# A GRU kernel's spline tail: slices written instead of added, and the spline moved into the recurrence's block

## The chip, the cores and the metric

The kernel runs on one core of one Trainium2 chip. The metric is the device time of one execution in microseconds (us); lower is better. The engines are TensorE (PE), VectorE (DVE), ScalarE (ACT), GpSimd (POOL) and SyncE (SP); SP and POOL issue nearly all transfers here.

## The reference

`x` has 4 batches, 1024 positions and 1024 features. A GRU with 1024 states runs over the positions, starting from `cond_2048`:

```python
gi = x @ W_ih + b_ih;  gh = h @ W_hh + b_hh
r = sigmoid(i_r + h_r);  z = sigmoid(i_z + h_z);  n = tanh(i_n + r * h_n)
h = (1 - z) * n + z * h            # hs[t] = h
```

Its states `hs` go through a routed spline layer. Each token is normalised (`xf = layernorm(hs) * gamma + beta`); the signs of `xf` choose one of 64 experts (best of 8 clusters, then best of 8 experts in it). Expert `k` owns the 16 features `16k` to `16k + 15`. `lo` and `hi` are the least and the greatest value of that slice over all tokens that chose the expert:

```python
u = clip((x_slice - lo) / (hi - lo + 1e-8), 0, 1 - 1e-6)
g = int(u * 16)                                    # cell of the 16-cell grid
delta = (base[k, j, g] + slope[k, j, g] * (u * 16 - g)) * output_scale[k]
out = x + hs;  out[token, 16k : 16k + 16] += delta
```

## The kernel before

The 1024 positions are cut into 16 chunks that run side by side (each warmed up over the 44 positions before it), so a step of the recurrence works on 16 x 4 = 64 columns in two sets (`s` = 0, 1) of 32. A `tile` is two steps of all columns: 128 tokens; there are `TILES` = 32 of them. Phases, in order of time:

- `input_product`: `x @ W_ih` into a scratch in HBM, and preparations.
- `recurrence`, one block of engine programs: warm-up steps, then `one_pass` over the 32 tiles. Tiles up to 21 run in `FULL` mode (three products with split weights), tiles 22 to 31 in `DIFFS` mode (one product, with stored sums of the warm-up added). Around the steps of tile `i` each engine does the routing work of the tiles before: ScalarE sums and squares (`act_sum`, `act_squares`, L734 to L740), GpSimd makes `rstd` and `shift` (`pool_scale`, L1109 to L1113), ScalarE normalises (L744), VectorE applies gamma and beta (`dve_signed`, L903 and L905), ScalarE takes signs (L749), VectorE finds the expert (`dve_route`, L920 to L932), TensorE turns the one-hot row (`pe_turn`, L636), ScalarE keeps it as `hits_t` (L753). GpSimd's `pool_keep` makes the row index and gathers the token's own slice of `hs` (L1134, 128 rows of 64 bytes), `pool_pick` copies it to `picks` (L1141), and `pool_add` adds the whole tile of `hs` to `y` by an accumulating transfer (L1120), after SP has copied `x` there (L1248, `begin_y`).
- `dve_ends` (L959 to L978) turns the picks into `records` (the slices of `xf`) and folds their ends into `ends`, in three batches of tiles and four parts each. The last batch is done after the last tile.
- `passes` (L563 to L573) wraps `one_pass`: after the first pass every engine loads `flag` (L566), and jumps over up to 16 further passes when it is 0, as it is here. Behind the jump the block ends, with a drain and a barrier (L573).
- `spline`, a second block: TensorE turns `ends` (L1414), VectorE reduces them to the experts' `lo` and `hi` and splits them into exact parts (L1452 to L1455, with `split_exactly`, L410 to L414). TensorE brings, through the one-hot rows, per-token values (`per_token`, L1430) and the curves of the token's expert (`curves(g)`, L1423; nine groups of 4 or 3 tiles; seven banks, in two halves: `curves(g)` waits until group `g - 2` is used). VectorE finds the cells (`cells(n)`, for tiles 0 to 3, 4 to 17 and 18 to 31) and, for each group, chooses among the 16 cells by halving (`choose(g)`, L1494) and makes `delta` (L1497 to L1500). GpSimd adds `delta` to `y`:

```python
            for g, (a, b) in enumerate(GROUPS):
                pool.wait_ge(delta_ready, g + 1)
                for i in range(a, b):
                    pool.indirect_dma_start(out=y_slices[:], out_offset=bass.IndirectOffsetOnAxis(ap=row_i[:, i:i + 1], axis=0),
                                            in_=delta[:, i], in_offset=None, compute_op=ALU.add).then_inc(added, 16)
            pool.wait_ge(added, 16 * TILES)
```

Each engine runs its own program in order; semaphores (`wait_ge`, `then_inc`) are the only order between engines. `curve_used` is sent by `value` (L1498), before the last multiplication.

Of the kernel before, what the change touches and what calls it, by code (L numbers as in the profile page):

```python
# [4 lines left out]
F32 = mybir.dt.float32  # L5
# [8 lines left out]
P = 128  # L14
# [7 lines left out]
SETS = 2  # L22
# [394 lines left out]
def recurrence(nc, ctx, t, h0, gi_dram, sums_dram, states_dram, hs_dram, x_rows, y_rows, tables, late_w):  # L417
# [3 lines left out]

    def pb(name, shape, dt=F32):
        return ctx.enter_context(nc.psum_tensor(name, shape, dt))
# [27 lines left out]
    pick_now = out_room[:, at + 7 * NT + 2 * ENDS_MOST:at + 7 * NT + 2 * ENDS_MOST + SLICE]  # L451
    affine_left = xhat[0:NT, D // 2:D // 2 + 4 * SLICE].rearrange("t (a f) -> t a f", a=2)
# [16 lines left out]
    n_act = sb("n_act", [P, SETS, QF])  # L469
    z_old = sb("z_old", [P, SETS, QF])  # L470
    new_n = n_sum
# [32 lines left out]
    affine_banks = affine[:].rearrange("p i f -> p (i f)")  # L504
    late_acc = [hit_bank[:], misc_bank[:], affine_banks[:, 0:512], affine_banks[:, 512:1024]]
# [67 lines left out]
    with nc.Block() as block:  # L573
# [75 lines left out]
        def _(pe):  # L649
# [45 lines left out]
            passes(pe, one_pass)  # L695

        def act_step(act, it, u, s, turns, mode=FULL, after_gates=None, after_tanh=None):
            n = steps_to(it, u)
            if mode == DIFFS:
                act.wait_ge(rz_done[s], n)  # L700
                nc.scalar.activation(rz[:, s], rz_bank[s][:], ACT.Sigmoid, scale=UNSCALE).then_inc(rz_ready[s], 1)
# [131 lines left out]
        def dve_step(dve, it, u, s, seeds, mode=FULL, after_sums=None, after_old=None):  # L833
# [7 lines left out]
            else:  # L841
                dve.wait_ge(rz_done[s], n)
                dve.wait_ge(gi_loaded[s][u], it * 64 + 64)
                nc.vector.scalar_tensor_tensor(out=sums[:, s, 0:RZ], in0=rz_bank[s][:], scalar=UNSCALE, in1=gi[:, s, u, 0:RZ],  # L844
# [136 lines left out]
        def _(dve):  # L981
# [50 lines left out]
            def one_pass(p, first):  # L1032
# [71 lines left out]
            passes(dve, one_pass)  # L1104

# [17 lines left out]
        def pool_keep(pool, T, tile):  # L1123
# [10 lines left out]
            pool.indirect_dma_start(out=pick_now[:], out_offset=None,  # L1134
                                    in_=hs_dram.rearrange("i q p (k j) -> (i q p k) j", j=SLICE),
                                    in_offset=bass.IndirectOffsetOnAxis(ap=row_now[:, 0:1], axis=0)).then_inc(picked, 16)

        def pool_pick(pool, T, tile):
            pool.wait_ge(picked, T * 16)
            pool.sem_inc(wait_carrier, 1)  # L1140
            nc.gpsimd.tensor_copy(t["picks"][:, one(tile)].rearrange("p o j -> p (o j)"), pick_now[:]).then_inc(pick_kept, 1)  # L1141

        @block.gpsimd
        def _(pool):
# [22 lines left out]
            def one_pass(p, first):  # L1167
# [190 lines left out]
def spline(nc, ctx, t, y_slices):  # L1358

    def sb(name, shape, dt=F32):  # L1360
        return ctx.enter_context(nc.sbuf_tensor(name, shape, dt))
# [25 lines left out]
    delta = sb("delta", [P, TILES, SLICE])  # L1387
# [7 lines left out]
    tok_bank = ctx.enter_context(nc.psum_tensor("tok_bank", [P, 512], F32))  # L1395
    turn_bank = tok_bank[0:NT, 4 * TILES:4 * TILES + 2 * P]
    curve_bank = ctx.enter_context(nc.psum_tensor("curve_bank", [P, 7, 512], F32))
# [3 lines left out]
    math_step, delta_ready, added = (sem(n) for n in ("math_step", "delta_ready", "added"))  # L1401
# [7 lines left out]
    with nc.Block() as block:  # L1409

        @block.tensor
        def _(pe):
# [215 lines left out]
```

## Time and profile before

| | us |
|---|---|
| median of 3 runs (2497.98 to 2498.7) | 2498.41 |
| the profiled execution | 2499.93 |
| its span, first to last instruction | 2498.1 |
| TensorE busy in the span | 2350.0 |
| VectorE busy | 1300.9 |
| ScalarE busy | 660.3 |
| GpSimd busy | 191.2 |

Busy times are of the profiled execution alone. They are averages over stages with different limits, so stretches have to be read one by one. The mean granted clock of TensorE is 0.966 of full speed.

### The profile page before, as it was taken

To read this page: it belongs to the slowest core of one execution; us is meant where nothing else is said; L and a number is where in the kernel's file an instruction comes from. 1 tells how busy PE (TensorE), PEld (TensorE's weight loads), DVE (VectorE), ACT (ScalarE), POOL (GpSimd) and SP (SyncE) were. 2 spreads that over 40 slices of the span, in tenths; PEclk is the share of its full clock that TensorE was granted. 3 is DMA by queue.
4 is the path that set the end of the run, shared out by engine and by line. 5 is a ranking of instruction groups with operands and counts; after the bars stand their busy time and mean duration, and the time that the engine had idled before them with its cause. 6 is when DMAs were issued, how large, how long until landed. Compare 5 with 4: busy or idle time off the path is not lost. (4 is left out here: it accounts for less than half of the span.)

```text
span 2498.1 us, 83612 instructions
## 1 busy us (share of the span) xinstructions
PE 2350.0 (94%) x35300; PEld 1285.8 (51%) x35300; DVE 1300.9 (52%) x2682; ACT 660.3 (26%) x1333; POOL 191.2 (8%) x376
## 2 busy tenths in 40 slices
PE   7999999999999989999999999999999999977734
PEld 3444444444444445455666666666666666544411
DVE  4322121212123357776666655666666666888865
ACT  3200000000001123333333323333333333355510
POOL 0000000000000000000000000111111111122217
PEclk9999999999999999999999999999999999999955
DMA  7693131313133445453444444444444444477712
GB/s 237 208 325 127 51 127 51 127 51 126 51 144 110 155 145 156 137 152 120 139 134 134 134 130 111 116 116 116 117 118 118 117 117 118 128 231 230 219 43 4
DMA packets 179895, 330.35 MB, mean 132 GB/s; under 512 B 27856, under 2 KB 89728, under 8 KB 178752
## 3 DMA queue, kind: packets, MB, share of 16 engines
q1 hardware_dynamic: 145360, 267.53, 34.0%
q10 hardware_dynamic: 24192, 44.05, 4.7%
q0 software_dynamic: 10240, 17.31, 4.7%
q8 instruction: 76, 1.25, 0.2%
q14 instruction: 27, 0.22, 0.0%
HBM read 222.13 MB, written 156.77 MB: 152 GB/s over the span
## 5 line engine op out<-in xcount | busy, mean ns | idle before, releaser
L580 PE MATMUL rz_bank<-w_hi,hi 128*32 128x512 f16 x6912 | 429.9, 392 | 49.4 <-DVE hi L879 37.0
L312 DVE SCALAR_TENSOR_TENSOR out_stage<-acc,bias_row 128x512 f32<-128x512 f32 x168 | 116.0, 690 | 624.4 <-PE acc L370 624.4
L368 PE MATMUL acc<-w_hi,x_even 128*128 128x512 f16 x768 | 291.8, 380 | 13.4 <-DVE x_even L304 11.3
L580 PEld LDWEIGHTS rz_bank<-w_hi,hi 128*32 128x32 f16 x6912 | 178.6, 99 | 234.4 <-DVE hi L879 45.3
L369 PE MATMUL acc<-w_hi,x_even 128*128 128x512 f16 x768 | 291.8, 380 | 0.0
L370 PE MATMUL acc<-w_lo,x_even 128*128 128x512 f16 x768 | 291.7, 380 | 0.0
L705 ACT ACTIVATE rz<-sums 128x512 f32<-128x512 f32 x176 | 110.9, 630 | 535.2 <-DVE sums L844 534.9
L844 DVE SCALAR_TENSOR_TENSOR sums<-rz_bank,stage 128x512 f32<-128x512 f32 x176 | 121.3, 689 | 239.3 <-PE rz_bank L580 239.2
L580 PE MATMUL rz_bank<-w_lo,hi 128*32 128x512 f16 x4096 | 243.2, 379 | 0.0
L580 PE MATMUL rz_bank<-w_hi,lo 128*32 128x512 f16 x4096 | 243.2, 379 | 0.0
L580 PE MATMUL n_bank<-w_hi,hi 128*32 128x256 f16 x6912 | 227.9, 274 | 0.0
L368 PE MATMUL acc<-w_hi,x_keep 128*128 128x512 f16 x576 | 218.3, 379 | 1.9 <-issue 1.9
L370 PE MATMUL acc<-w_lo,x_keep 128*128 128x512 f16 x576 | 218.3, 379 | 0.0
L369 PE MATMUL acc<-w_hi,x_keep 128*128 128x512 f16 x576 | 218.3, 379 | 0.0
L580 PEld LDWEIGHTS n_bank<-w_hi,hi 128*32 128x32 f16 x6912 | 186.2, 98 | 53.6 <-issue 5.3
L580 PEld LDWEIGHTS rz_bank<-w_lo,hi 128*32 128x32 f16 x4096 | 109.6, 97 | 84.2
L580 PEld LDWEIGHTS rz_bank<-w_hi,lo 128*32 128x32 f16 x4096 | 109.6, 97 | 84.1
L710 ACT ACTIVATE n_act<-n_sum 128x256 f32<-128x256 f32 x216 | 90.2, 417 | 178.7 <-DVE n_sum L857 178.7
L580 PE MATMUL n_bank<-w_lo,hi 128*32 128x256 f16 x4096 | 134.0, 273 | 0.0
L580 PE MATMUL n_bank<-w_hi,lo 128*32 128x256 f16 x4096 | 134.0, 273 | 0.0
L368 PEld LDWEIGHTS acc<-w_hi,x_even 128*128 128x128 f16 x768 | 75.3, 98 | 104.8 <-issue 12.1
L580 PEld LDWEIGHTS n_bank<-w_lo,hi 128*32 128x32 f16 x4096 | 109.6, 97 | 29.5
(191 smaller groups left out, 2661.6 us busy)
## 6 DMA issues: line engine op xcount, KB each, us to landing
stage<-gi_scratch SPq DMA_DIRECT2D x704, 96.0 KB
gi_scratch<-out_stage ACTq DMA_DIRECT2D x168, 256.0 KB, 2.0
stage<-sums_scratch SPq DMA_DIRECT2D x40, 512.0 KB
stage<-in_xT SPq DMA_DIRECT2D x32, 512.0 KB, 6.3
y<-in_x_rows SPq DMA_DIRECT2D x32, 512.0 KB, 4.4
hs_scratch<-h SPq DMA_DIRECT2D x128, 128.0 KB
x_keep<-hs_scratch SPq DMA_DIRECT2D x32, 512.0 KB, 3.9
y<-hs_scratch POOLq DMA_DIRECT2D x32, 512.0 KB, 7.7
```

The lines of the kernel that those rows point to most:

```text
L312: nc.vector.scalar_tensor_tensor(out=out_stage[:, tb], in0=acc[e % BANKS][:], scalar=UNSCALE, in1=bias_row[:].rearrange("p q f -> p (q f)" ...
L368: nc.tensor.matmul(acc[e % BANKS][:], hi, wh, start=k == 0, stop=False)
L369: nc.tensor.matmul(acc[e % BANKS][:], lo, wh, start=False, stop=False)
L370: last = nc.tensor.matmul(acc[e % BANKS][:], hi, wl, start=False, stop=k == KB - 1)
L580: last = nc.tensor.matmul(bank[q * COLS:(q + 1) * COLS, 0:b - a], state[:, s, j], w[:, j, q * QW + a:q * QW + b], start=first and j == 0, ...
L705: nc.scalar.activation(rz[:, s], sums[:, s, 0:RZ], ACT.Sigmoid).then_inc(rz_ready[s], 1)
L710: nc.scalar.activation(n_act[:, s], n_sum[:, s], ACT.Tanh).then_inc(n_ready[s], 1)
L844: nc.vector.scalar_tensor_tensor(out=sums[:, s, 0:RZ], in0=rz_bank[s][:], scalar=UNSCALE, in1=gi[:, s, u, 0:RZ], op0=ALU.mult, op1=ALU.add ...
```

## The change

The spline no longer has a block of its own: `spline` returns three functions, `pe_spline`, `dve_spline` and `pool_spline`, and each engine's program in the recurrence's block calls its own behind `passes`. Its tiles lie in `w_lo`, its PSUM banks are the recurrence's. A new semaphore `ends_ready` stands between VectorE's last ends and TensorE's transposes; `curves(0)` now precedes that wait. The scatter writes the slice and no longer accumulates; what it has to hold, `x + hs + delta`, VectorE makes with one more addition per group from `base`. `base` is gathered in the main pass: `pool_keep` issues a second gather, of `x`, and `pool_pick` adds the two. GpSimd waits for the last add to `y` before it leaves the pass. In the last tile's work the order changes: GpSimd keeps tile 30 and scales before it adds to `y`, and VectorE does `dve_ends(p, 1, 1)` before `dve_signed`.

```diff
 def recurrence(...):
+    x_now = out_room[:, at + 8 * NT:at + 8 * NT + SLICE]
+    base = t["base"]
...
-    rz_bank = [pb(f"rz_bank{s}", [P, 512]) for s in range(SETS)]
-    n_bank = [pb(f"n_bank{s}", [P, 512]) for s in range(SETS)]
-    hit_bank = pb("hit_bank", [P, 512])
-    misc_bank = pb("misc_bank", [P, 512])
-    affine = pb("affine", [P, TILES, 2 * SLICE])
+    banks = t["banks"]
+    rz_bank = [banks[:, s] for s in range(SETS)]
+    n_bank = [banks[:, SETS + s] for s in range(SETS)]
+    hit_bank, misc_bank = banks[:, 4], banks[:, 5]
+    affine = banks[:, 6:8].rearrange("p b f -> p (b f)").rearrange("p (i f) -> p i f", f=2 * SLICE)
...
             passes(pe, one_pass)
+            pe_spline(pe)
...
+                dve_ends(dve, p, 1, 1)
                 dve_signed(dve, T)
-                dve_ends(dve, p, 1, 1)
                 dve_route(dve, T)
...
             passes(dve, one_pass)
+            dve_spline(dve)
...
         def pool_keep(pool, T, tile):
...
-            pool.indirect_dma_start(out=pick_now[:], out_offset=None,
-                                    in_=hs_dram.rearrange("i q p (k j) -> (i q p k) j", j=SLICE),
-                                    in_offset=bass.IndirectOffsetOnAxis(ap=row_now[:, 0:1], axis=0)).then_inc(picked, 16)
+            for now, rows in ((pick_now, hs_dram), (x_now, x_rows)):
+                pool.indirect_dma_start(out=now[:], out_offset=None,
+                                        in_=rows.rearrange("i q p (k j) -> (i q p k) j", j=SLICE),
+                                        in_offset=bass.IndirectOffsetOnAxis(ap=row_now[:, 0:1], axis=0)).then_inc(picked, 16)
...
         def pool_pick(pool, T, tile):
-            pool.wait_ge(picked, T * 16)
+            pool.wait_ge(picked, T * 32)
             pool.sem_inc(wait_carrier, 1)
+            nc.gpsimd.tensor_tensor(base[:, one(tile)].rearrange("p o j -> p (o j)"), x_now[:], pick_now[:], ALU.add)
...
-                with pool.Fori(2, TILES + 1) as i:
+                with pool.Fori(2, TILES) as i:
                     tile(i, True)
+                T = p * TILES + TILES
+                pool_keep(pool, T - 1, TILES - 2)
+                pool_scale(pool, T, TILES - 1)
+                pool_add(pool, T, TILES - 1)
+                pool_pick(pool, T - 1, TILES - 2)
                 pool_keep(pool, p * TILES + TILES, TILES - 1)
                 pool_pick(pool, p * TILES + TILES, TILES - 1)
+                pool.wait_ge(y_added, p * (TILES * 16) + TILES * 16)
+                pool.sem_inc(wait_carrier, 1)
 
             passes(pool, one_pass)
+            pool_spline(pool)
...
 def spline(nc, ctx, t, y_slices):
 
+    room = t["w_lo"][:].rearrange("p k n -> p (k n)")
...
-    delta = sb("delta", [P, TILES, SLICE])
+    delta = rise
...
-            for e in range(2):
-                ins = nc.tensor.transpose(turn_bank[:, e * P:(e + 1) * P], t["ends"][:, e], t["ident"][:])
-            ins.then_inc(ends_turned, 1)
...
+    def pe_spline(pe):
...
+        curves(0)
+        pe.wait_ge(ends_ready, 1)
+        for e in range(2):
+            ins = nc.tensor.transpose(turn_bank[:, e * P:(e + 1) * P], t["ends"][:, e], t["ident"][:])
+        ins.then_inc(ends_turned, 1)
+        pe.wait_ge(rows_split, 1)
+        per_token(*CELLS[0])
...
+    def dve_spline(dve):
...
+        dve.sem_inc(ends_ready, 1)
+        dve.wait_ge(ends_turned, 1)
...
-                nc.vector.tensor_tensor(delta[:, s], value[:, s], wide(per_tok[:, s, 0]), ALU.mult).then_inc(delta_ready, 1)
+            step(nc.vector.tensor_tensor(delta[:, s], value[:, s], wide(per_tok[:, s, 0]), ALU.mult))
+            nc.vector.tensor_tensor(delta[:, s], t["base"][:, s], delta[:, s], ALU.add).then_inc(delta_ready, 1)
...
-                                            in_=delta[:, i], in_offset=None, compute_op=ALU.add).then_inc(added, 16)
+                                        in_=delta[:, i], in_offset=None).then_inc(added, 16)
...
 def program(...):
+        t["base"] = ctx.enter_context(nc.sbuf_tensor("base", [P, TILES, SLICE], F32))
+        t["banks"] = ctx.enter_context(nc.psum_tensor("banks", [P, BANKS, 512], F32))
...
-        t["records"] = ctx.enter_context(nc.sbuf_tensor("records", [P, TILES, SLICE], F32))
+
+        t["records"] = t["picks"]
...
-                       y, tables, late_w)
-        with ExitStack() as phase:
-            spline(nc, phase, t, y.rearrange("i q p (k j) -> (i q p k) j", j=SLICE))
+                       y, tables, late_w, *spline(nc, phase, t, y.rearrange("i q p (k j) -> (i q p k) j", j=SLICE)))
```

## Rows read from the trace of the kernel before

**Rows 1.** Windows: stretch, length, then busy us (count) per engine, clock, DMA share.
```profile
1520.00:2180.00 660.00, 658.09 (x16058) 429.31 (x16046) 446.91 (x970) 244.14 (x504) 81.03 (x204) 1.00 0.45 118
2180.00:2384.00 204.00, 153.15 (x2626) 79.10 (x2626) 170.25 (x417) 113.13 (x278) 45.92 (x100) 0.90 0.76 220
2433.00:2475.00 42.00, 32.24 (x75) 10.30 (x73) 33.98 (x91) 0.00 (x0) 34.37 (x22) 0.50 0.22 5
```

**Rows 2.** The chain that ended last: start us, us, engine, what, line.
```profile
2419.55 0.60 PE tok_bank L1414 x2
...
2441.75 1.54 POOL y L1513
...
2492.02 1.55 POOL y L1513
```

**Rows 3.** Timeline of the spline: start us, us, engine, line, what, idle before.
```profile
2432.69 0.22 DVE L1500 TENSOR_TENSOR delta<-value,per_tok 128x64 f32<-128x64 f32 x1
...
2441.29 18.10 PE L1423 MATMUL curve_bank<-curve_parts,late_ring 64*128 64x512 bf16 x42 [3.28 <-DVE value L1498]
...
2471.18 2.75 DVE L1494 COPY_PREDICATED curve_bank<-in_upper,curve_bank 128x1024 f32<-128x1024 int32 x4 [2.14 <-PE curve_bank L1423]
...
2474.49 0.22 DVE L1500 TENSOR_TENSOR delta<-value,per_tok 128x64 f32<-128x64 f32 x1
```

**Rows 4.** Groups of GpSimd's indirect transfers, and their medians of us to landing.
```profile
L1513 POOL DMA_INDIRECT y<-delta,row_i x32 | 49.9, 1559 | 33.9 <-DVE delta L1500 24.7 <-issue 9.1
...
L1134 POOL DMA_INDIRECT late_out<-hs_scratch,row_now x30 | 33.5, 1117 | 19.2 <-issue 19.2
...
late_out<-hs_scratch,row_now POOLq DMA_INDIRECT x32, 2.5
y<-delta,row_i POOLq DMA_INDIRECT x32, 3.0
```

**Rows 5.** Timeline: the last row part, and the first per-token products.
```profile
2421.60 0.16 DVE L414 CAST row_parts<-row_left 64x4 bf16<-64x4 f32 x1
...
2425.18 0.50 PE L1430 MATMUL tok_bank<-row_parts,late_ring 64*128 64x4 bf16 x12
```

**Rows 6.** Queue instructions by line: duration ns, then first and last start us.
```profile
L566 PEldq COMPARE_BRANCH  x1: 3640/3640/3640, 2406.2 to 2406.2; - x1
...
L566 DVEq COMPARE_BRANCH  x1: 56/56/56, 2415.6 to 2415.6; - x1
...
L573 DVEq DRAIN  x1: 76/76/76, 2419.2 to 2419.2; - x1
```

**Rows 7.** Timeline behind the last tile's steps.
```profile
2393.28 0.15 DVE L1095 CAST flag<-misc_bank 1x1 int32<-1x1 f32 x1 [0.68 <-PE misc_bank L690]
...
2395.16 0.19 POOL L1113 TENSOR_TENSOR shift<-neg_mean,rstd 128x1 f32 x1 [0.16 <-POOL rstd L1111]
...
2396.66 1.23 DVE L903 TENSOR_TENSOR x_keep<-x_keep,gamma_s 128x1024 f32<-128x1024 f32 x1 [3.23 <-ACT x_keep L744]
...
2401.63 1.22 DVE L920 TENSOR_REDUCE late_out<-bias_row 128x64 f32<-128x1024 bf16 x1
...
2409.62 0.19 POOL L1141 COPY picks<-late_out 128x16 f32<-128x16 f32 x1 [2.69 <-DMA late_out<-hs_scratch,row_now]
...
2413.96 0.22 DVE L978 TENSOR_TENSOR ends<-late_out,ends 128x64 f32<-128x64 f32 x1
```

**Rows 8.** Timeline: two rows of a `FULL` tile, then three of a `DIFFS` tile.
```profile
1913.44 0.19 POOL L1113 TENSOR_TENSOR shift<-neg_mean,rstd 128x1 f32 x1 [0.17 <-POOL rstd L1111]
...
1918.47 1.23 ACT L744 ACTIVATE x_keep<-x_keep,shift,rstd 128x1024 f32<-128x1024 f32 x1
...
2293.72 1.16 POOL L1134 DMA_INDIRECT late_out<-hs_scratch,row_now  x1 [0.46 <-issue]
...
2296.30 0.19 POOL L1113 TENSOR_TENSOR shift<-neg_mean,rstd 128x1 f32 x1 [0.16 <-POOL rstd L1111]
...
2299.48 1.22 DVE L903 TENSOR_TENSOR x_keep<-x_keep,gamma_s 128x1024 f32<-128x1024 f32 x1
```

More of the change, by code:

```diff
@@ L1 @@
+import math
 import concourse.bass as bass
@@ L1358, in spline @@
 def spline(nc, ctx, t, y_slices):
+    room = t["w_lo"][:].rearrange("p k n -> p (k n)")
+    taken = [0]
     def sb(name, shape, dt=F32):
-        return ctx.enter_context(nc.sbuf_tensor(name, shape, dt))
+        halves = math.prod(shape[1:]) * (1 if dt == BF16 else 2)
+        flat = room[0:shape[0], taken[0]:taken[0] + halves].bitcast(dt)
+        taken[0] += (halves + 15) // 16 * 16
+        dims = "abc"[:len(shape) - 1]
+        return flat.rearrange(f"p ({' '.join(dims)}) -> p {' '.join(dims)}", **dict(zip(dims, shape[1:])))
     def sem(name):
@@ L1394, in spline @@
     CELLS = ((0, 4), (4, 18), (18, TILES))
-    tok_bank = ctx.enter_context(nc.psum_tensor("tok_bank", [P, 512], F32))
+    tok_bank = t["banks"][:, 7]
     turn_bank = tok_bank[0:NT, 4 * TILES:4 * TILES + 2 * P]
-    curve_bank = ctx.enter_context(nc.psum_tensor("curve_bank", [P, 7, 512], F32))
+    curve_bank = t["banks"][:, 0:7]
     ends_turned, row_step, rows_split, tok_ready, tok_known, curve_ready, curve_used = (
         sem(n) for n in ("ends_turned", "row_step", "rows_split2", "tok_ready", "tok_known", "curve_ready", "curve_used"))
-    math_step, delta_ready, added = (sem(n) for n in ("math_step", "delta_ready", "added"))
+    math_step, delta_ready, added, ends_ready = (sem(n) for n in ("math_step", "delta_ready", "added", "ends_ready"))
     def curves_of(g):
@@ new lines, in pe_spline, with curves, per_token @@
+    def pe_spline(pe):
+        def curves(g):
+            if g >= 2:
+                pe.wait_ge(curve_used, g - 1)
+            a, b = GROUPS[g]
+            for i in range(a, b):
+                for part in range(3):
+                    ins = nc.tensor.matmul(curve_bank[:, 4 * (g % 2) + i - a], hits_t[:, i], curve_parts[:, part],
+                                           start=part == 0, stop=part == 2)
+            ins.then_inc(curve_ready, 1)
+        def per_token(a, b):
+            for i in range(a, b):
+                for part in range(3):
+                    ins = nc.tensor.matmul(tok_bank[:, i * 4:(i + 1) * 4], hits_t[:, i], row_parts[:, part],
+                                           start=part == 0, stop=part == 2)
+            ins.then_inc(tok_ready, 1)
+        curves(0)
[5 more added lines that the diff above has]
+        per_token(*CELLS[0])
+        pe.wait_ge(tok_known, 1)
+        per_token(CELLS[0][1], TILES)
+        for g in range(1, len(GROUPS)):
+            curves(g)
@@ L1518, in constants, with pool_spline @@
+    def pool_spline(pool):
+        for g, (a, b) in enumerate(GROUPS):
+            pool.wait_ge(delta_ready, g + 1)
+            for i in range(a, b):
+                pool.indirect_dma_start(out=y_slices[:], out_offset=bass.IndirectOffsetOnAxis(ap=row_i[:, i:i + 1], axis=0),
+                                        in_=delta[:, i], in_offset=None).then_inc(added, 16)
+        pool.wait_ge(added, 16 * TILES)
+    return pe_spline, dve_spline, pool_spline
 def constants(nc, t):
```

152 lines of the change are left out of this document (57 added, 95 removed).

## The prediction

> **What bounds the kernel now.** I read the windows view first, to cut the run into stages [rows 1]. From 1520 to 2180 us TensorE is busy 658 of 660 us at full clock: the main pass over tiles 1 to 21 (the `FULL` mode) is TensorE's. From 2180 to 2384 (the `DIFFS` tiles 22 to 31) TensorE is busy 153 of 204 and VectorE 170. From 2433 on TensorE's granted clock is 0.50, its 1.2 GHz level; behind the last tile, from about 2384, lies a tail of 114 us. The first two stages can only lose by this change unless a wait in them goes; the gain has to come from the tail.
>
> In the tail I read the chain that ended last [rows 2]. It starts at the spline's first transposes at 2419.55, goes through one group of curve products, VectorE's `cells(0)`, `choose(0)`, `cells(1)`, `choose(1)`, and from 2441.75 it is GpSimd alone: 28 issues of the accumulating scatter of L1513. The reader is to see the cadence: 1.55 us of issue and 0.30 us between, 1.86 us each. VectorE made its last `delta` at 2474.71 [rows 3], 17.3 us before the last scatter began, so VectorE and TensorE are not the bound there.
>
> The spans: the profiled execution took 2499.93 us for a span of 2498.1, so 1.8 us lie outside; the median of the runs is 2498.41, 1.5 below the profiled one. I sum differences on the profiled one and take them from the median. A difference of 0.2% is 5.0 us, about what a measurement of this kernel tells from none.
>
> **1. The scatter's price.** `compute_op=ALU.add` goes; 32 scatters of 128 rows of 64 bytes stay. The trace has no plain scatter. Its nearest rows are the accumulating scatter, 1559 ns mean, and the plain gather of the same 128 x 64 bytes on the same engine, 1117 ns mean [rows 4]. The landing is 3.0 us after the issue's start for the one and 2.5 for the other. So an issue costs between 1.10 and 1.55 us. I take 1.10: the gather differs in the side that has the index, the scatter in a second read of the destination for the sum, and the latter is what the change takes away. The 0.30 us between issues stays. Cadence: 1.40 (or 1.86 at the other end). A page of the Trainium skill speaks for less: "DMA: Bandwidth & Descriptors" (its table at the top) says that a transfer under 512 bytes is read-modify-write anyway. No row tells whether that hits a plain 64-byte write; by it the landing would stay 3.0 instead of 2.5 and the end come 0.5 us later.
>
> **2. What the scatters then wait for.** From the first `delta` (2432.91, end) to the last (2474.71) VectorE takes 41.8 us [rows 3]. The change puts one addition (`base` to `delta`, 128x64) in each of nine groups: 0.22 + 0.03 us by L1500's row [rows 3]. Replayed against TensorE: `curve_used` is sent before the multiplication by the scale, so TensorE is not delayed; the groups whose curves VectorE waits for anyway (4, and 8 with 2.14 us of waiting [rows 3]) absorb it. What is left at the last group is 0.26 us that the extra addition of group 4 puts on `cells(2)` and what follows, and its own 0.26: 42.3 us from first to last `delta`. GpSimd has 24 scatters to issue from group 1's arrival (its first began at 2441.75 [rows 2], 8.8 us behind group 0's `delta`) to group 8's: 24 x 1.40 = 33.6 us against 42.3 - 8.8 = 33.5. So at 1.40 GpSimd just keeps up, and the last scatter starts at 0.3 (hop) + 42.3 + 3 x 1.40 = 46.8 us after the first `delta`; before it was 2492.02 - 2432.91 = 59.1. That is **-12.3**. A cheaper scatter than 1.40 would bring only its last three. At 1.86 nothing is gained here (+0.3, the extra addition in group 1).
>
> **3. Behind the last scatter.** Before, 6.1 us from its start to the end. With the landing at 2.5 instead of 3.0: **-0.5**. The drain and what else lies behind stay.
>
> **4. Curves early.** `curves(0)` (12 products, 5.2 us at the 0.43 us of 42 in 18.10 [rows 3]) stood between the transposes and the per-token products, which began at 2425.18 though VectorE had `row_parts` at 2421.76 [rows 5]. Now it runs while VectorE still makes the ends: TensorE's conditional jump begins at 2406.2 and takes 3.64 us [rows 6], then 5.2 us: done by 2415. The per-token products follow `row_parts` at once (a hop of 0.06): 3.42 - 0.07 = **-3.35**. The extra addition in `choose(0)` gives back **+0.26**.
>
> **5. The block's boundary.** VectorE's last step ends at 2414.18 [rows 7] and the transposes start at 2419.52. One would book these 5.3 us as the barrier of the block. The queue rows tell otherwise [rows 6]: VectorE loads the flag and compares it until 2415.65, and its next instruction, the drain, is at 2419.2: 3.55 us behind the taken branch. TensorE's branch shows the same as its own length, 3.64 us. The branch over the conditional passes is still there and is as far, so 5.0 of the 5.3 stay; the drain and the semaphores go: **-0.2** (0.1 is the new `ends_ready` hop). The Trainium skill says this of a taken branch ("Runtime: NRT & Kernel Launch", Instruction fetch mechanics): a target outside the fetched window has to be fetched by DMA first. By it and by the row the boundary gives 0.2; by the barrier alone it would give 5.2.
>
> **6. The recurrence's end, reordered** [rows 7]. VectorE idled 3.23 us from the flag (2393.43) until `xhat` came. `dve_ends(1, 1)` filled the 2.5 us from the end of `dve_signed` (2396.66 and two operations of 1.23) to the routing at 2401.63; now it fills that idle time, to about 2396.0. GpSimd now keeps tile 30 before it adds to `y`, so `shift` has neither that issue nor a wait for its input before it: it came at 2395.35 and is wanted, for `dve_signed` at 2396.0, by 2394.7. I take it that it gets there. Then `dve_signed` ends at 2398.5, ScalarE's signs take at most the 1.23 us of its pass over the same shape (L744, [rows 8]), and the routing starts at 2399.7 instead of 2401.63: 1.9 us sooner. But GpSimd now gathers twice for the last tile too: from the routing's start to the kept picks (2409.81) it took 8.2 us, now 8.2 + 1.40 (second issue) + 0.25 (the addition, by the copy's 0.19 and a pause) = 9.85 from 2399.7, so 2409.55. The last ends wait for the picks. Of 1.9 us **-0.25** stays.
>
> **7. The second gather in the main pass.** It stands in `pool_keep`, before `pool_scale` on GpSimd's queue; behind `pool_scale` waits ScalarE's normalisation (L744), and in ScalarE's queue the next gate behind that. In `FULL` tiles `shift` is there 4.8 us before its use [rows 8], 1.4 is hidden. In `DIFFS` tiles GpSimd goes from the gather straight to `var_eps`, so the gather is already what `shift` waits for, and 1.17 + 0.30 = 1.47 us more comes through. `shift` ends at 2296.49; normalisation (1.23) must end before VectorE reads at 2299.48: slack 1.68 [rows 8]. 1.47 fits, with 0.2 left; with the 0.46 us pause that the first gather has before it, it would just fit. If the second issue cost what the accumulating scatter does, 1.86, 0.18 us would come through in each of ten tiles: +2. I take 0 and keep +2. The additions of `base` lie in GpSimd's idle time (46 of 204 us busy [rows 1]). The wait for `y_added` on GpSimd ends long before the first `delta`.
>
> `delta = rise`, `records = picks`, the tiles in `w_lo` and the renamed banks cost nothing: same shapes, same engines.
>
> **Sum.** -12.3 - 0.5 - 3.35 + 0.26 - 0.2 - 0.25 = -16.3: 2498.41 - 16.3 = **2482.1 us**.
>
> **Rivals.**
> A. *The plain scatter costs what the accumulating one did.* For: it is the side with the index that may set the price, and no row has that alone. Then steps 2 and 3 give +0.3 and 0: -3.2, 2495.2 us. A price between (issues of 1.25 to 1.45 us) makes GpSimd the bound from group 1 on, with 27 cadences: 2.7 us for each 0.1, so 2486 to 2492.
> B. *The boundary goes*: the code behind the branch is fetched already when VectorE gets there, against the 3.55 and 3.64 us of [rows 6]. For: part of these could be the next block's code, which now is laid elsewhere. Then 3.5 us more: 2478.6.
> C. *Slower: the second gather in the `DIFFS` tiles.* It comes a few us behind the 512 KB add to `y`, on the same queue. If GpSimd had to wait for room there, `shift` would be late, and VectorE with it: per tile (cost - 1.68), ten times. To eat 16.3 + 5.0 us it would need to cost 3.8 us, to only come out slower 3.3 us. Against: the first gather, at the same place, costs 1.16 there [rows 8] and 1.12 in the mean [rows 4].
> D. *TensorE gets its full clock back in the tail*, because `curves(0)` now fills an idle stretch. Then groups 4 and 8 need not wait; group 8's 2.14 us is the most that it gives. Against: 42 products in 18.1 us did not raise it from 0.50 [rows 3].
>
> **Chances.** The forecast with its small unknowns (D and up to +2 of step 7 among them) 0.65; A in full 0.12; A in part 0.13; B 0.07; C 0.03. The likeliest case's own range is 2479.5 to 2485. For the whole, from B's 2477.5 up to 2490.5, which leaves out A in full, a little of A in part, and C. Faster by over 0.2% (below 2493.4): 0.65 + 0.13 + 0.07 = 0.85; within 0.2%: A in full, less a little, 0.11; slower 0.04.
>
> **What would show it.** Step 1: L1513's row, mean about 1.1 us and landings of 2.5; near 1.55 is A. Step 2: the last scatters wait for VectorE's last addition, not for "issue"; last scatter about 46.5 us behind the first. Step 4: the per-token products begin within 0.2 us of the last `row_parts`. Step 5: from the last end to the transposes 5.1 us; under 3 is B. Step 6: the routing's start 1.9 us sooner, the last ends only 0.25. Step 7: the `DIFFS` tiles take 204 us as before, and L903 with no idle time before it; if it waits for L744, the slack was used up. What makes me wrong most easily is the price of a plain scatter, the one number no row has.

## The result and the profile after

The changed kernel takes **2480.85 us** (median of 6 runs, 2479.73 to 2484.99) beside 2498.55 (6 runs, 2497.57 to 2498.82) for the kernel before: ratio 0.9933, 95% interval 0.9923 to 0.9943, so 17.7 us less. The forecast was 2482.1. The profiled execution took 2479.73 us for a span of 2478.2.

Four numbers cut a profile: the start of GpSimd's first add to `y` (the main pass is then at its first tile), the start of the first scatter, the start of the last, and the span.

| | first `y` add | first scatter | last scatter | span |
|---|---|---|---|---|
| before | 1519.63 | 2433.21 | 2492.02 | 2498.08 |
| after | 1516.46 | 2426.42 | 2472.47 | 2478.16 |

The scatters' stretch went from 58.81 to 46.05 us (-12.8), what lies behind it from 6.06 to 5.69 (-0.4), and the stretch from the first add to `y` to the first scatter from 913.6 to 910.0 (-3.6). The other 3.2 us lie in the setup, which the change does not touch; three other profiles of the changed kernel have 1518.5, 1518.2 and 1517.6 there, so most of that part is chance.

The windows view of after, with the columns of [rows 1]:
```profile
1520.00:2180.00 660.00, 655.94 (x15990) 425.33 (x15982) 448.48 (x974) 246.29 (x508) 103.78 (x243) 1.00 0.45 118
2180.00:2384.00 204.00, 138.72 (x2610) 75.43 (x2602) 169.80 (x414) 113.07 (x274) 57.52 (x120) 0.97 0.76 219
2427.00:2469.00 42.00, 31.20 (x73) 9.92 (x71) 34.72 (x96) 0.00 (x0) 27.20 (x29) 0.50 0.03 6
```
Of the work, only GpSimd's changes in the first two stretches (81 to 104 us, 46 to 58: the second gather and `base`). TensorE's 139 us instead of 153 in the second stretch go with its granted clock, 0.97 in this execution and 0.90 in the one of before. That did not make the `DIFFS` tiles shorter: 20.6 us in both. In the tail the clock stays at 0.50.

The scatters in the grouped view, with the columns of [rows 4]:
```profile
L1530 POOL DMA_INDIRECT y<-w_lo,row_i x32 | 31.3, 978 | 35.7 <-DVE w_lo L1518 27.2 <-issue 8.5
```
The view of one line has its instructions' duration in ns (least, median, most), their first and last start and the time to landing. Of the scatter's line and of the gathers':
```profile
L1530 POOL DMA_INDIRECT y<-w_lo,row_i x32: 955/962/1173, 2426.4 to 2472.5; - x32
...
DMA to landing us min/median/max: 2.1/2.1/2.7
...
L1138 POOL DMA_INDIRECT late_out<-hs_scratch,row_now x32: 1067/1115/1204, 1560.6 to 2401.5; - x32
L1138 POOL DMA_INDIRECT late_out<-in_x_rows,row_now x32: 953/958/1525, 1562.1 to 2402.9; - x32
```
Against [rows 4] a scatter costs 978 instead of 1559 ns, and lands 2.1 instead of 3.0 us after its issue starts. With the 0.30 us between issues, the cadence (from one issue's start to the next's) is 1.27.

The timeline of the spline after, to be laid beside [rows 2] and [rows 3]:
```profile
2425.91 0.23 DVE L1518 TENSOR_TENSOR w_lo<-base,w_lo 128x64 f32<-128x64 f32 x1
...
2435.15 0.96 POOL L1530 DMA_INDIRECT y<-w_lo,row_i  x1 [3.90 <-DVE w_lo L1518]
...
2455.55 0.21 DVE L1518 TENSOR_TENSOR w_lo<-base,w_lo 128x48 f32<-128x48 f32 x1
...
2456.03 0.96 POOL L1530 DMA_INDIRECT y<-w_lo,row_i  x1 [2.99 <-DVE w_lo L1518]
...
2468.06 0.22 DVE L1518 TENSOR_TENSOR w_lo<-base,w_lo 128x64 f32<-128x64 f32 x1
...
2472.47 0.96 POOL L1530 DMA_INDIRECT y<-w_lo,row_i  x1 [0.30 <-issue]
```
L1518 is now the last operation of each group. GpSimd waits for it twice, at group 1 (3.90 us) and at group 5 (2.99); from 2456.03 on it issues the last 14 scatters without a wait. The last `delta` ends at 2468.28, and three cadences behind it and a hop of 0.3 (from VectorE's end to GpSimd's start) give 2472.4, which is where the last scatter is anyway. So both engines set the end: VectorE up to group 5, and from there either.

The timeline ahead of the spline, TensorE and one row of VectorE, to be laid beside [rows 5] and [rows 7]:
```profile
2405.31 5.30 PE L1436 MATMUL banks<-curve_parts,late_ring 64*128 64x512 bf16 x12 [4.29 <-issue]
...
2410.56 0.22 DVE L980 TENSOR_TENSOR ends<-late_out,ends 128x64 f32<-128x64 f32 x1
...
2415.86 0.63 PE L1450 MATMUL banks<-ident,ends 128*64 128x128 f32 x2 [5.25 <-DVEq L1467]
...
2418.15 0.48 PE L1443 MATMUL banks<-w_lo,late_ring 64*128 64x4 bf16 x12 [1.66 <-DVE w_lo L416]
```
`curves(0)` is done at 2410.6, before the last end is. The per-token products follow the last row part (started at 2417.93) at 2418.15. From the last end to the transposes there are 5.08 us, 5.34 before.

### The profile page after: what moved, and what is told of

Its sections match the earlier page's. It is cut to its first block and busy times, and to the rows that moved or that the text cites. A ratio compares the mean times of both kernels' runs of the same rounds, so it can differ in the third digit from the quotient of the medians.

```text
span 2478.2 us, 83692 instructions
## 1 busy us (share of the span) xinstructions
PE 2335.3 (94%) x35300; PEld 1277.8 (52%) x35300; DVE 1303.3 (53%) x2691; ACT 661.4 (27%) x1333; POOL 210.6 (8%) x440
## 5 line engine op out<-in xcount | busy, mean ns | idle before, releaser
L581 PE MATMUL banks<-w_hi,hi 128*32 128x512 f16 (+1 forms) x13824 | 605.0, 328 | 55.7 <-DVE hi L881 43.0
L581 PEld LDWEIGHTS banks<-w_hi,hi 128*32 128x32 f16 x13824 | 359.8, 97 | 284.8 <-DVE hi L881 53.7
L581 PE MATMUL banks<-w_hi,lo 128*32 128x512 f16 (+1 forms) x8192 | 354.9, 326 | 0.0
L581 PE MATMUL banks<-w_lo,hi 128*32 128x512 f16 (+1 forms) x8192 | 354.9, 326 | 0.0
L370 PE MATMUL acc<-w_hi,x_even 128*128 128x512 f16 x768 | 291.7, 380 | 13.5 <-DVE x_even L306 11.1
L581 PEld LDWEIGHTS banks<-w_lo,hi 128*32 128x32 f16 x8192 | 217.8, 97 | 115.0
L581 PEld LDWEIGHTS banks<-w_hi,lo 128*32 128x32 f16 x8192 | 217.8, 97 | 115.0
L846 DVE SCALAR_TENSOR_TENSOR sums<-banks,stage 128x512 f32<-128x512 f32 x176 | 121.5, 690 | 238.3 <-PE banks L581 238.2
L370 PEld LDWEIGHTS acc<-w_hi,x_even 128*128 128x128 f16 x768 | 75.3, 98 | 104.7 <-issue 11.7
L371 PEld LDWEIGHTS acc<-w_hi,x_even 128*128 128x128 f16 x768 | 75.3, 98 | 90.6 <-issue 0.6
L871 DVE TENSOR_TENSOR n_sum<-not_z,n_act 128x256 f32<-128x256 f32 x216 | 92.6, 429 | 36.8 <-ACT n_act L712 36.8
L886 DVE TENSOR_TENSOR h<-n_sum,z_old 128x256 f32<-128x256 f32 x216 | 90.3, 418 | 20.4 <-DVE n_sum L871 7.4
```

What stands on the lines that cost most here:

```text
L370: nc.tensor.matmul(acc[e % BANKS][:], hi, wh, start=k == 0, stop=False)
L371: nc.tensor.matmul(acc[e % BANKS][:], lo, wh, start=False, stop=False)
L581: last = nc.tensor.matmul(bank[q * COLS:(q + 1) * COLS, 0:b - a], state[:, s, j], w[:, j, q * QW + a:q * QW + b], start=first and j == 0, ...
L871: nc.vector.tensor_tensor(new_n[:, s], not_z[:, s], n_act[:, s], ALU.mult).then_inc(new_n_ready[s], 1)
L886: nc.vector.tensor_tensor(h_new, new_n[:, s], z_old[:, s], ALU.add).then_inc(h_ready[s], 1)
```

## Experiments

The runs were made in three sets, each on a chip of its own (1st, 2nd, 3rd). On which chip the first measurement was made is not recorded. Ratios are against the kernel before on the same chip. A `FULL` tile's time is the mean from the add to `y` of tile 2 to that of tile 21, a `DIFFS` tile's from tile 22 to tile 30, counted from 0; the expectations below leave out the two longer tiles at the end of the `FULL` mode and have 31.5 and 32.5 for 31.75 and 32.73. "Behind it" is from the start of the last scatter to the end of the span.

| run | median us | ratio, 95% interval | us per `FULL` tile | first to last scatter | behind it |
|---|---|---|---|---|---|
| changed, 1st chip | 2500.47 | 1.0009 (1.0000 to 1.0018) | 32.73 | 46.20 | 5.69 |
| accumulating, one gather | 2495.16 | 0.9986 (0.9977 to 0.9996) | 31.76 | 58.82 | 8.80 |
| plain scatter in before | 2484.58 | 0.9942 (0.9927 to 0.9958) | 31.76 | 45.70 | 5.21 |
| curves late | 2503.49 | 1.0022 (1.0013 to 1.0031) | 32.73 | 46.04 | 5.69 |
| changed, 2nd chip | 2481.14 | 0.9929 (0.9914 to 0.9944) | 31.74 | 46.19 | 5.69 |
| one gather | 2484.11 | 0.9939 (0.9924 to 0.9954) | 31.75 | 46.15 | 7.86 |
| `hs` gathered twice | 2481.35 | 0.9930 (0.9915 to 0.9945) | 31.76 | 46.19 | 5.69 |
| `x` behind the scale | 2479.80 | 0.9924 (0.9910 to 0.9937) | 31.76 | 46.20 | 5.73 |
| changed, 3rd chip | 2480.28 | 0.9927 (0.9912 to 0.9942) | 31.75 | 46.19 | 5.69 |
| no branch | 2475.90 | 0.9909 (0.9894 to 0.9924) | 31.78 | 46.21 | 5.68 |
| three gathers | 2496.34 | 0.9992 (0.9982 to 1.0001) | 31.77 | 46.19 | 7.48 |
| ends sent early | 2479.39 | 0.9922 (0.9908 to 0.9935) | 31.76 | 46.20 | 5.73 |

### The scatter's form alone, both ways

In the kernel before, the scatter made plain (its slices then hold the spline's part alone, without `x + hs`):
```
-    in_=delta[:, i], in_offset=None, compute_op=ALU.add)
+    in_=delta[:, i], in_offset=None)
```


> The kernel before, with compute_op taken from its scatter and nothing else; its slices hold delta alone, without x and hs. Theory (price of accumulating): issues of 0.96 us and a landing of 2.1 us here too; the first scatter starts at the same place, VectorE's groups come when they came, so the last scatter is set by group 5 (its delta ended 29.3 us behind group 0's) plus 13 x 1.27 or by the last delta (41.8) plus 3 x 1.27: 46 us from first to last instead of 58.8, and 0.35 less behind it. 2498.5 - 12.8 - 0.35 = 2485.3. Rival (place): issues stay 1.55 and the time 2498.5.

Measured: 13.5 us less than before, first to last scatter 45.70. In the changed kernel, the accumulating scatter put back, with the second gather and `base` taken out, so that the sum is whole again:

> The changed kernel with the scatter accumulating again, and without the second gather, the addition that makes base and the nine additions of base; it computes the same output. Theory: what the change brought in the scatters was the price of accumulating, 0.59 us of each. Then issues are 1.55 us again, 1.86 from one to the next, the scatters are GpSimd's from group 1 on, 58.6 us from first to last, and 6.1 from the last to the end: 12.6 + 0.4 us slower than the changed kernel, less about 1.5 for the last tile's single gather and 0.7 for the main pass: 2480.85 + 10.8 = 2491.7. Rival: the scatters are cheaper because they stand in the recurrence's block or because their data and indices lie elsewhere; then they stay at 0.96 us and the time is 2479.

Measured: 2495.16, 2.9 us less than before; the scatters cost what they did before:
```profile
L1528 POOL DMA_INDIRECT y<-w_lo,row_i x32 | 49.9, 1560 | 30.3 <-DVE w_lo L1516 21.2 <-issue 9.1
```
So the price belongs to the form of the scatter (plain 0.98 us also in the old code, accumulating 1.56 also in the new). By itself the form is worth 13.5 us in the old code, beside the 17.7 of the whole change in the first measurement, whose profile has 13.1 for the scatters' stretch and what lies behind it. The miss of the second run is not in the scatters (58.82, as expected) but behind them: 8.80 us instead of 6.06. The queue rows name it. GpSimd's last drain, by itself, in that run, in the run with one gather, and in the changed kernel:
```profile
L574 POOLq DRAIN  x1: 5338/5338/5338, 2489.2 to 2489.2; - x1
```
```profile
L574 POOLq DRAIN  x1: 5338/5338/5338, 2478.6 to 2478.6; - x1
```
```profile
L574 POOLq DRAIN  x1: 3174/3174/3174, 2474.8 to 2474.8; - x1
```
It goes with the program: 5338 ns in both kernels with one gather in the block, 3174 in all with two gathers at L1138, 4971 with three, 3215 with the second gather placed elsewhere; before, 5297 at the end of the recurrence's block, with its one gather, and 2660 at the end of the spline's own. There the longer one cost nothing: it was over at 2416.0, ahead of VectorE's drain at 2419.2. In the changed kernel's single block GpSimd's drain is the last thing that runs. What in the program sets it was not tried.

### Curves late

```
     def pe_spline(pe):
-        curves(0)
         pe.wait_ge(ends_ready, 1)
```
with the call put back between the transposes and the per-token products.

> The changed kernel with curves(0) moved back between the transposes and the per-token products. Theory: the 5.3 us of 12 products come back into the chain from the transposes to the first scatter, of which 1.6 us lie beside VectorE's reductions and splits, less hops: 3.4 us slower, 13.9 from the transposes to the first scatter instead of 10.6; all behind it unchanged: 2484.3. Rival: the products may be slower or faster after the idle time that arises (TensorE's granted clock is 0.50 in both); then the 10.6 moves by another amount, or the scatters' stretch of 46.1 does.

Measured: 3.0 us more than the changed kernel on the same chip. From the transposes to the first scatter 13.94 us instead of 10.56, the 3.4 that step 4 says.

### The changed kernel on other chips

> The changed kernel once more, beside the kernel before on the same chip. In the first pair of profiles the main pass began 3.2 us sooner in the changed kernel (first add to y at 1516.5 against 1519.6), in a part that the change does not touch. Theory 1 (chance of one execution): it begins at about 1519.5 here, or anywhere between, and the tail's terms (last ends to transposes 5.1, transposes to first scatter 10.6, first to last scatter 46.1, then 5.7) are the same within 0.1 us. Theory 2 (the new layout of the tiles makes the setup faster): it begins at 1516.5 again.

Measured: nothing gained, 2500.47 us. The tail is as it was (46.20 and 5.69). The 20 us are in the main pass: the first add to `y` at 1518.5, the one of tile 21 at 2204.5 instead of 2182.6. The timeline of one `FULL` tile on this chip, GpSimd and TensorE:
```profile
1855.43 1.10 POOL L1138 DMA_INDIRECT late_out<-hs_scratch,row_now  x1 [0.69 <-issue]
...
1856.84 0.96 POOL L1138 DMA_INDIRECT late_out<-in_x_rows,row_now  x1 [0.30 <-issue]
...
1857.48 0.13 PEld L581 LDWEIGHTS banks<-w_lo,hi 128*32 128x32 f16 x6 [0.56 <-issue]
...
1858.23 0.80 PEld L581 LDWEIGHTS banks<-w_lo,hi 128*32 128x32 f16 x19 [0.62 <-issue]
```
The weight loads stop twice, next to the issue of the second gather, with no semaphore that the trace names ("issue"), at a granted clock of 1.00. Each `FULL` tile has these two stops, and is 0.98 us longer for them (32.73 against 31.75), 20 tiles. The two kernels with one gather on this chip have none; curves late, with two, has them. The same kernel on two more chips:

> The changed kernel, a third time. In its second run its FULL tiles took 32.5 us instead of 31.5, with two stops of 0.65 and 0.7 us in TensorE's weight loads in each tile, the first within 0.05 us of the second gather's issue; in its first run no such stop. Theory 1 (it goes with the chip or with where the data lie on it): here it is one of the two, 2481 or 2500, for all executions alike. Theory 2 (chance from execution to execution): single times on both sides.

> The changed kernel once more, beside the runs of this call, on whichever chip this is. Two profiles of it so far show FULL tiles of 31.5 us and a ratio of 0.993, one shows 32.5 us with two stops of TensorE's weight loads (0.65 and 0.70 us) in each and a ratio of 1.001. Theory 1 (the stops go with the chip): all profiles and times of this call show the one or the other. Theory 2 (they come and go by chance with each run): the runs of this kernel in this call are spread by over 10 us.

Measured: 2481.14 and 2480.28 us, no stops, 31.75 us a tile, as in the first measurement. The runs of each set agree (2480.32 to 2481.61, 2479.18 to 2481.11; on the chip with the stops 2499.14 to 2504.96), so the stops go with the set, that is with the chip or with something that stayed the same on it (where the data lie, say), and not with the single run. One chip of three had them, and it was met in one set only.

### What the second gather costs

One gather (the second left out, `base` made from `hs` alone, so `x` is missing in the slices), and `hs` gathered twice (the same, with both issues):
```
-            for now, rows in ((pick_now, hs_dram), (x_now, x_rows)):
+            for now, rows in ((pick_now, hs_dram), (x_now, hs_dram)):
```


> The changed kernel without the second gather (base becomes twice the slice of hs, so the written slices lack x); every other part stays. Theory A (the second gather makes TensorE's stops): no stop in any FULL tile wherever it runs, tiles of 31.5 us; the last tile's picks come 0.7 to 1.4 us sooner: 2479.5. Theory B (the stops come from the new layout of tiles and banks, or from the longer program, and only coincide with the gather): where the changed kernel has them beside it, this has them too.

> The changed kernel with the second gather reading hs again instead of x (the written slices lack x). Theory A1 (what stops TensorE is the second indirect issue itself, or two of them back to back): it goes as the changed kernel beside it, 2481 or 2500. Theory A2 (it is the source x, where it lies in memory): no stops here even where the changed kernel has them, 2481.

Measured: one gather 2484.11, 3.0 us slower than with two; `hs` twice 2481.35, the same as the changed kernel. The 3.0 do not come from the gather's own place. 2.2 us are the drain above (7.86 against 5.69). The first add to `y` is 3.6 us later in that profile, in the setup; but the profiled execution took 2485.78, and two of the four took 2482.6 and 2482.8, so how much of this is in the median is open. From the add of tile 30 to the first scatter, one gather is 1.5 us faster (56.36 against 57.87). The `DIFFS` tiles are 20.58 us with one gather and with two. On this chip the tensor gathered from makes no difference. There were no stops to remove here, and on the chip that has them neither kernel was tried. Nor does the tensor set an issue's price. Two issues of one tile, both from `hs`:
```profile
1751.64 1.10 POOL L1138 DMA_INDIRECT late_out<-hs_scratch,row_now  x1 [0.70 <-issue]
1753.05 0.95 POOL L1138 DMA_INDIRECT late_out<-hs_scratch,row_now  x1 [0.30 <-issue]
```
The one right behind another costs 0.95; with the gather of `x` moved away from that of `hs` (the run with `x` behind the scale) it costs 1.06 in such a tile.

Three gathers (a third, `x` again, into a buffer that nothing reads):
```
-            for now, rows in ((pick_now, hs_dram), (x_now, x_rows)):
+            for now, rows in ((pick_now, hs_dram), (x_now, x_rows), (x_more, x_rows)):
```


> The changed kernel with a third gather of each tile, x's slice once more, right behind the second, into a buffer that nothing reads; nothing else differs. Theory 1 (rival C's mechanism: GpSimd's gathers are what shift waits for in the DIFFS tiles, with a slack of 1.68 us of which the second gather used up 1.27): the third costs 1.27 again, 0.85 us of it comes through in each of ten DIFFS tiles, TensorE waits for the normalisation there, and the kernel takes 8 us more than the changed kernel of this call (plus up to 1.2 for the last tile's picks). FULL tiles stay at 31.5 (slack 4.8). Theory 2 (the normalisation is not on the path in the DIFFS tiles even then): within 1.5 us of the changed kernel. If this is a chip with the stops of TensorE: they come with every gather behind the first (three in each FULL tile, 33.0 us or more) or stay two (32.5).

Measured: 16.1 us more than the changed kernel, twice what was expected. A `DIFFS` tile takes 21.59 instead of 20.56 us. ScalarE's and VectorE's rows of the normalisation in the window 2180 to 2384 (busy us, mean ns, then idle us before them and for whom), first with two gathers (the first measurement), then with three:
```profile
L746 ACT ACTIVATE x_keep<-x_keep,shift,rstd 128x1024 f32<-128x1024 f32 x10 | 12.4, 1240 | 2.5 <-POOL shift L1116 1.4
...
L905 DVE TENSOR_TENSOR x_keep<-x_keep,gamma_s 128x1024 f32<-128x1024 f32 x10 | 12.2, 1215 | 0.7 <-ACT x_keep L746 0.7
```
```profile
L747 ACT ACTIVATE x_keep<-x_keep,shift,rstd 128x1024 f32<-128x1024 f32 x9 | 11.2, 1241 | 14.9 <-POOL shift L1117 14.9
...
L906 DVE TENSOR_TENSOR x_keep<-x_keep,gamma_s 128x1024 f32<-128x1024 f32 x9 | 11.0, 1225 | 8.4 <-ACT x_keep L747 8.4
```
The third gather costs 1.26 us (from one issue's start to the next's, 2299.66 to 2300.92 in the timeline), and 1.03 of it come through in each tile: the second had left 0.23 us of slack. With three gathers VectorE waits 0.93 us in each tile. With two it waits 0.7 us once in ten tiles in the first measurement, and not at all in the profiles of the 2nd and 3rd chip. The granted clock, 0.90 in this stretch with three gathers and 0.98 with two on this chip, is not the cause: it was 0.90 in the kernel before too, with tiles of 20.6 us. From the add of tile 21 to that of tile 30 the profile is 8.3 us longer than the changed kernel's; from there to the add of tile 31 another 4.3 (27.0 against 22.7), where `shift` is late again, to the first scatter 1.1, and the drain gives 1.8. Rival C's mechanism is real and was 0.2 us away.

### The branch

The conditional passes (the correction passes that put the running sums right) taken out:
```
         body(0, True)
-        eng.wait_ge(pass_judged, 1)
-        eng.sem_inc(wait_carrier, 1)
-        with eng.If(eng.value_load(flag[0:1, 0:1], min_val=0, max_val=P) > 0):
-            ...
```


> The changed kernel with the branch over the conditional passes taken out, and with it these passes, which set the running sums right where tiles are not in order; nothing else differs. The prediction's step 5 says that 5.0 us between VectorE's last end and the first transpose are VectorE's load of the flag, its comparison (1.5 us) and the 3.55 us behind the taken branch. Theory 1 (it is the branch and the fetch behind it): from the last end to the transposes 0.2 instead of 5.1 us, 4.9 us faster than the changed kernel of this call. Theory 2 (the 3.55 us are the fetch of code that VectorE needs anyway, branch or none): the load and comparison go, 1.5 us, and some 3.5 us stay.

Measured: 4.4 us less than the changed kernel on that chip. VectorE's last end and the transposes:
```profile
2411.81 0.23 DVE L972 TENSOR_TENSOR ends<-late_out,ends 128x64 f32<-128x64 f32 x1
...
2412.15 0.64 PE L1442 MATMUL banks<-ident,ends 128*64 128x128 f32 x2 [4.77 <-DVEq L1459]
```
0.11 us between them instead of 5.25 in the changed kernel on that chip: load, comparison and the 3.5 us behind the taken branch belong to the branch. The code behind it has to come in either case; without the branch nothing waits for it. The DMA view of the changed kernel (first measurement) from VectorE's branch to its next work, 2412.2 to 2415.8, has two transfers, both of instructions:
```profile
q14 instruction: 2, 0.02, 2.1%
```
Without the branch, from 2411.9 to 2412.3, where VectorE's last end meets the transposes, there is none.

### Two ways to hide the rest

The second gather placed behind GpSimd's scaling of the normalisation, with a semaphore of its own, so that it is no longer ahead of `shift`:

> The changed kernel with x gathered behind pool_scale, with a semaphore of its own, and the picks kept before x is waited for; it computes the same output. In FULL tiles the second gather begins some 2.5 us later. Theory A1 with the place in time: if the gather stops TensorE wherever it falls, the stops move with it, to another weight load, and the time is that of the changed kernel beside it less 2; if it is the gathers back to back, or that one place in TensorE's stream, the stops are gone and it is 2479 on every chip. Without stops it should beat the changed kernel by 1.2 us (the last tile's picks no longer wait for x: VectorE idled 1.25 us for them) and the 0.7 us that the one late shift took in a DIFFS tile: 2479.

Measured: 2479.80 us, 1.3 below the changed kernel on that chip, by intervals that overlap. The last tile's gather of `x` has nothing ahead of it to hide behind and still follows that of `hs` at once, but the picks no longer wait for it: VectorE waits for them 0.51 instead of 1.25 us. That, and VectorE's signal moved ahead of its branch:
```
                 for part in range(4):
                     dve_ends(dve, p, 2, part)
+                dve.sem_inc(ends_ready, 1)
```


> The changed kernel with two moves. The gather of x's slice stands behind GpSimd's scaling of the normalisation, with a semaphore of its own (as in the run with x behind the scale, 2479.8 us); and TensorE waits for the last ends and turns them ahead of its branch, so that the transposes lie under VectorE's branch. Theory 1 (between the last end and the spline's first choice VectorE's own branch is the bound, and only TensorE's transposes, the split row parts' copies and the hops behind ends_ready come off): 0.75 us less than with x behind the scale alone, 2479.0 us; TensorE's first transpose stands 0.2 us behind the last end instead of 5.1. Theory 2 (TensorE, turned early, starts its own branch later, and its 3.6 us fetch ends behind VectorE's): nothing gained or up to 0.5 us lost. If this is a chip with the stops of TensorE: they either go, because the second gather is away from the first (31.5 us a FULL tile), or move with it.

The expectation says more than the edit does: TensorE's wait in the spline stayed where it was, behind its own branch and `curves(0)`, so the transposes are not ahead of its branch; only VectorE's signal moved (the wait that TensorE got ahead of its branch is in the further passes alone, which do not run). Measured: 2479.39 us, 0.9 below the changed kernel on that chip, again within the intervals.
```profile
2410.19 0.29 DVE L980 TENSOR_TENSOR bias_row<-bias_row,late_out 128x128 f32<-128x128 bf16 x1
...
2411.17 0.23 DVE L984 TENSOR_TENSOR ends<-late_out,ends 128x64 f32<-128x64 f32 x1
2416.44 0.28 DVE L1487 TENSOR_REDUCE rows<-banks 64x1 f32<-64x128 f32 x1 [5.05 <-issue]
```
From the last end to the first reduction of the transposed bank 5.04 us instead of 5.92 in the changed kernel on that chip (5.75 and 5.72 in the first measurement and on the 2nd chip), with the transposes at 2412.08, as `curves(0)` ends. So 0.7 to 0.9 us are gained there; what is left is VectorE's branch alone ("issue", no longer TensorE's bank). No time of a whole run tells this version from the changed kernel; its profile does.

## Why the prediction was right

2482.1 was forecast and 2480.85 came. The profile's own parts give -12.8 - 0.4 - 3.6 = -16.8 without the setup, the forecast's sum was -16.3. The mechanism was right in its main terms, the plain scatter and the early curves. That the sum is this close is in part luck: steps 2, 3, 6 and 7 each have an error, and they nearly cancel.

**Step 1, the scatter's price.** Taken 1.10 + 0.30 us, measured 0.98 in the mean (0.96 the median) + 0.30. The gather was the right neighbour, and the accumulation was what cost more. What the step missed is that the gather it took stood alone: right behind another an issue costs 0.96 in the median, gather and plain scatter alike. Rival A is out, by both runs on the scatter's form. The landing fell too, from 3.0 to 2.1 us. The step had read the rule of the Trainium skill ("DMA: Bandwidth & Descriptors", Specifications) as one by which it would stay 3.0; that price does not show. Whether a plain write of 64 bytes is a read-modify-write all the same, these rows do not tell.

**Step 2, what the scatters wait for.** First to last `delta` 42.14 us (42.3 forecast), last scatter 46.05 us behind the first (46.5). The number is right, the sentence "GpSimd just keeps up" is not. It looked at group 1 and at the last group alone and missed the place where GpSimd is held up, at group 5, whose `delta` comes late behind `cells(2)`: it ended 29.6 us after the first one. At a cadence of 1.40 the 13 cadences behind it would have given 0.3 + 29.6 + 18.2 = 48.1 us, not 46.8. The scatter's lower price, 1.27, made up for it: 0.3 + 29.6 + 16.4 = 46.3. That is luck. "A cheaper scatter than 1.40 would bring only its last three" is wrong for the same reason: it brought the last 13.

**Step 3, behind the last scatter.** -0.5 forecast, -0.4 came, from two terms: the landing gave 0.9, and "the drain and what else lies behind stay" was wrong, the drain grew from 2660 to 3174 ns.

**Step 4, curves early.** -3.09 with what it gives back; -3.13 from the transposes to the first scatter, and 3.4 when undone.

**Step 5, the boundary.** -0.2 forecast, -0.26 came. Rival B is out. Here the rule of the Trainium skill ("Runtime: NRT & Kernel Launch", Instruction fetch mechanics) and the rows agree: two transfers of instructions lie in VectorE's wait, and the run without the branch has 0.11 us in place of some 5; merging the blocks alone took 0.26.

**Step 6, the recurrence's end.** From the flag to the routing 6.32 us instead of 8.35: -2.03, forecast -1.93. From the routing to the kept picks 9.1, forecast 9.85. The term for the second gather was too large: the step added its whole 1.40 us to the wait for the first gather's landing. In fact its issue lies under that wait: from the first issue's start to the landing of all there are 4.5 us (2401.53 to 2406.05) against 3.8 before. So -1.09 of -2.03 stayed, forecast -0.25: 0.84 us too little.

**Step 7, the second gather in the main pass.** 0 forecast; `FULL` 31.75 and `DIFFS` 20.6 us a tile as before, in the first measurement and on two of three chips. Yet steps 4, 5 and 6 add up to -4.5 and only -3.6 came: in the first measurement's profile the main pass, from the first add to the flag, takes 874.5 us instead of 873.7. The greater part of that is one tile in which the slack was used up and VectorE waited:
```profile
2358.81 1.23 DVE L905 TENSOR_TENSOR x_keep<-x_keep,gamma_s 128x1024 f32<-128x1024 f32 x1 [0.69 <-ACT x_keep L746]
```
The profiles of the 2nd and 3rd chip have no such wait and 874.0 and 873.8 us. The step had 0.2 us left, from a slack of 1.68 and a price of 1.47. Measured, the price is 1.26 and 0.23 is left, as the three gathers show; so the slack is 1.49, and both terms were 0.2 too large. On the 1st chip the step is wrong by 20 us, and no row of the trace of before shows it coming.

**Rival D**: the clock stayed at 0.50.

**What stays open.** Why TensorE's weight loads stop on that one chip. Shown: of the four kernels run there, the two with a second gather have the stops and the two without have none, and no kernel has them on the 2nd or 3rd chip. TensorE's own instructions are the same in the kernel with one gather and the accumulating scatter, which has no stops. That kernel also lacks GpSimd's addition that makes `base`, so the gather is not the only thing taken out; that it causes the stops is argued from their place beside its issue. Open too is what sets the length of GpSimd's last drain, which made the run with the accumulating scatter 2.7 us longer than the kernel before at its end. Whether a gather moved elsewhere would avoid them was not tried there: the kernel with `x` behind the scale ran on another chip.

## What to carry to other kernels

Where an indirect scatter accumulates into rows that only it touches, gather the old value early and write plainly: here 0.58 us for each of 32 issues on the path, for one more gather of 1.26 us a tile in idle time. Work out each place where a queue can run dry, not only the first and the last: here the one that mattered was the last group that came late, with 13 issues still behind it. An issue added to an engine ahead of something small that others wait for is free only up to the slack; measure how much is left by issuing it once more, and time the kernel on more than one chip.

## What was not expected of the hardware

- An accumulating indirect scatter of 128 rows of 64 bytes takes 1.56 us to issue, a plain one 0.98, and they land 3.0 and 2.1 us after their start. A plain gather takes 1.06 to 1.20 us, and right behind another 0.96 in the median, from either tensor (the last tile's took 1.52). Queue q0 has 10240 packets before and 6656 with the plain scatter alone: 112 fewer for each of 32 scatters.
- GpSimd's drain at the end of a block takes 2.66 to 5.34 us. It is 3174 ns in each of the four profiles of the changed kernel, and changes when instructions far ahead of it do.
- Behind the taken branch over the conditional passes VectorE's next work comes some 3.5 us later; without the branch 0.11 us lie between the last end and the transposes instead of some 5.
- On one chip of three, TensorE at a granted clock of 1.00 stops twice in each `FULL` tile, 0.56 and 0.62 us, beside GpSimd's second indirect issue.
